# Cross attention with the queries on partitions: maxima from the scores themselves, weights transposed by DMA

## What is computed

```
xn = layernorm(ctx[b])                       # 1444 x 128
q  = (layernorm(x1[b]) @ Wq) * (1+scale) + shift
k, v = split(xn @ Wkv)
p  = softmax(q_h . k_h * 64**-0.5)            # for each head h: 100 x 1444
out = concat_h(p @ v_h) @ Wout;   x2[b] = layernorm(x1[b] + out)
```

## Time and profile before

| | us |
|---|---|
| median of 3 runs | 1530.29 (1527.89 to 1530.91) |
| profiled execution, its own time | 1527.42 |
| its span (first to last instruction) | 1525.6 |
| TensorE busy | 1356.7 (89%) |
| VectorE busy | 1162.8 (76%) |
| ScalarE busy | 857.3 (56%) |
| GpSimd busy | 625.4 (41%) |

### The profile page before, as it was taken

How to read it: one execution, slowest core, us unless ns; L and a number is a source line. 1 busy time by engine, 2 the same in 40 slices (tenths; PEclk the granted TensorE clock), 3 DMA queues, 4 the chain that set the end, 5 groups by cost and what they waited for, 6 DMA issues and landing times. The chain is left out here.

```text
span 1525.6 us, 28851 instructions
## 1 busy us (share of the span) xinstructions
PE 1356.7 (89%) x9254; PEld 835.3 (55%) x9254; DVE 1162.8 (76%) x3204; ACT 857.3 (56%) x1346; POOL 625.4 (41%) x419
## 2 busy tenths in 40 slices
PE   2769999999999999999999999999999753888888
PEld 2644555555555555555555555555555452777778
DVE  5967787777877787787777777777876328999994
ACT  0445676757667675767667575757665553222221
POOL 3243654636463554646364554636463300000010
PEclk9768999999999999999999999999999966666666
DMA  6020110101010110101010010101010110000000
GB/s 135 1 41 1 41 41 1 42 3 41 1 41 22 22 41 2 42 1 41 2 41 26 17 42 1 41 3 22 1 22 1 41 51 0 2 5 5 5 5 9
DMA packets 67469, 34.32 MB, mean 22 GB/s; under 512 B 53332, under 2 KB 64888, under 8 KB 67192
## 3 DMA queue, kind: packets, MB, share of 16 engines
q1 hardware_dynamic: 67320, 32.33, 9.2%
HBM read 18.92 MB, written 0.82 MB: 13 GB/s over the span
## 5 line engine op out<-in xcount | busy, mean ns | idle before, releaser
L800 POOL TENSOR_TENSOR p_lo<-e,p_hi 128x800 f16<-128x800 f32 x208 | 386.2, 1864 | 437.6 <-ACT p_hi L881 436.7
L928 DVE TENSOR_REDUCE mxp<-ps 128x1 f32<-128x481 f32 (+3 forms) x624 | 398.2, 654 | 153.1 <-PE ps L1040 141.4
L878 ACT ACTIVATE e<-ps 128x800 f32<-128x800 f32 (+1 forms) x384 | 324.7, 846 | 217.3 <-PE ps L1084 217.2
L881 ACT ACTIVATE p_hi<-ps 128x800 f16<-128x800 f32 (+1 forms) x384 | 325.2, 847 | 0.0
L1097 PE MATMUL ps<-p_hi,xa_hi 128*128 128x400 f16 (+1 forms) x768 | 256.3, 334 | 8.2 <-ACT p_hi L881 6.4
L1082 PE MATMUL ps<-q_hi,xT_hi 128*128 128x400 f16 (+1 forms) x768 | 257.6, 335 | 5.3 <-ACT p_hi L881 4.5
L1083 PE MATMUL ps<-q_lo,xT_hi 128*128 128x400 f16 (+1 forms) x768 | 256.0, 333 | 0.0
L1084 PE MATMUL ps<-q_hi,xT_lo 128*128 128x400 f16 (+1 forms) x768 | 256.0, 333 | 0.0
L1101 PE MATMUL ps<-p_lo,xa_hi 128*128 128x400 f16 (+1 forms) x768 | 255.1, 332 | 0.3
L1098 PE MATMUL ps<-p_hi,xa_lo 128*128 128x400 f16 (+1 forms) x768 | 255.1, 332 | 0.0
L1040 PE MATMUL ps<-xT_hi,q_hi 128*128 128x481 f16 (+3 forms) x624 | 236.4, 379 | 6.4 <-DMA xT_hi<-xa_hi 2.2
(11 more groups left out here) (223 smaller groups left out, 1948.0 us busy)
## 6 DMA issues: line engine op xcount, KB each, us to landing
raw<-in_ctx SPq DMA_DIRECT2D x16, 704.0 KB
f_wq<-in_L_ffn_w_q SPq DMA_DIRECT2D x1, 1024.0 KB, 6.3
f_wqt<-in_ffn_wq_t SPq DMA_DIRECT2D x2, 512.0 KB, 7.8
x_tok<-in_x SPq DMA_DIRECT2D x1, 800.0 KB
out_x<-ost SPq DMA_DIRECT2D x6, 128.0 KB, 1.9
wk_t<-in_wk_t SPq DMA_DIRECT2D x1, 512.0 KB, 5.9
wq_t<-in_wq_t SPq DMA_DIRECT2D x1, 512.0 KB, 8.2
wv_t<-in_wv_t SPq DMA_DIRECT2D x1, 512.0 KB, 10.5
```

The lines of the kernel that those rows point to most:

```text
L800: pool.tensor_tensor(out=p_lo[t % P_SLOTS][0:r, :, :], in0=e32[t % E_SLOTS][0:r, :, :], in1=p_hi[t % P_SLOTS][0:r, :, :], op=ALU.subtract) ...
L878: act.activation(e32[t % E_SLOTS][0:r, :, :], s_banks(t, r), ACT.Exp).then_inc(exp_done, 1)
L881: act.activation(p_hi[t % P_SLOTS][0:r, :, :], s_banks(t, r), ACT.Exp).then_inc(exp_done, 1)
L928: dve.tensor_reduce(mxp[0:r, mt, c:c + 1], src[0:r, 0:MCUT[c + 1] - MCUT[c]], AX_X, ALU.max).then_inc(work_dve, 1)
```

## The change

The queries go on partitions. A batch has 13 query tiles (NM), 12 of 128 queries and a last one of 64; the last computes the scores of 128 but uses only partitions 64 to 127. One tile's scores are 128 queries x 1444 keys in three PSUM banks (two sets of three), so VectorE reduces the maximum along the free direction from the scores themselves, adds 6.0 and ScalarE takes the exponent with this as its bias, once, as fp32. The high half is a copy of it, the low half the difference as before (GpSimd for tiles 1, 4, 7, 10, else VectorE). High and low half stand in one buffer `p` of 128 x 3072, which one transposing DMA turns into `pT`, 24 blocks with the keys on partitions. The values then take 36 matmuls of 128 columns a tile, five tiles behind the scores, in one bank; a copy to `uT` is made for every four tiles. The side work for the maxima is gone, queries and outputs use one bank. The loop is gone too: all 208 tiles are written out. Cut to its core:

```diff
-    body(Batch(None, 0), True, False)
-    with eng.Fori(0, (B - 2) // 2) as i:
-        body(Batch(i, 1), False, False)
-        body(Batch(i, 2), False, False)
-    body(Batch(None, B - 1), False, True)
...
+LAG = 5
+RING = 6
+E_BUF, P_BUF, N_BUF = 2, 3, 4
+GT = 4
+POOL_LO = (1, 4, 7, 10)
+Q_SLOTS = (2, 3, 7, 8)
+Y_SLOTS = (9, NM, NM + 1, NM + 4, NM + 5, NM + 6)
...
+            def turn_weights(t):
+                rows = tile_rows(t % NM)
+                sp.wait_ge(lo_pool if t % NM in POOL_LO else lo_dve, lo_of(t))
+                if t >= RING:
+                    sp.wait_ge(pv_done, t - RING + 1)
+                sp.dma_start_transpose(pT[:, t % RING, :, 0:rows.stop - rows.start],
+                                       p[t % P_BUF][rows, :, :].rearrange("q h k -> q (h k)")).then_inc(pT_ld[t % RING], 16)
...
+            for t in range(ALL_TILES):
+                b, i = divmod(t, NM)
+                turn_weights(t)
+                if i == 6 and b + 3 < B:
+                    sp.wait_ge(xh_done, b + 2)
+                    context_load(sp, cx, a, Batch(None, b + 3))
+                if i == 7 and b + 1 < B:
+                    turn_context(b + 1, 0, xa_hi_done)
+                if i == 8 and b + 1 < B:
+                    turn_context(b + 1, 1, xa_lo_done)
...
+            def low_half(t):
+                rows = tile_rows(t % NM)
+                pool.wait_ge(hi_done, t + 1)
+                pool.tensor_tensor(out=p[t % P_BUF][rows, 1, 0:T], in0=e32[t % E_BUF][rows, :], in1=p[t % P_BUF][rows, 0, 0:T],
...
+            def exponent(t):
+                rows = tile_rows(t % NM)
+                act.wait_ge(bias_done, t + 1)
+                if t >= E_BUF:
+                    act.wait_ge(lo_pool if (t - E_BUF) % NM in POOL_LO else lo_dve, lo_of(t - E_BUF))
+                act.activation(e32[t % E_BUF][rows, :], score_banks(t)[rows, 0:T], ACT.Exp,
+                               bias=bias[rows, t % N_BUF:t % N_BUF + 1]).then_inc(e_done, 1)
+
+            def high_half(t):
+                rows = tile_rows(t % NM)
+                if t >= P_BUF:
+                    act.wait_ge(pT_ld[(t - P_BUF) % RING], 16 * ((t - P_BUF) // RING + 1))
+                act.wait_ge(e_done, t + 1)
+                act.activation(p[t % P_BUF][rows, 0, 0:T], e32[t % E_BUF][rows, :], ACT.Copy).then_inc(hi_done, 1)
...
+            for t in range(ALL_TILES + DRAIN):
+                b, i = divmod(t, NM)
+                if t < ALL_TILES:
+                    exponent(t)
+                v = t - LAG
+                if 0 <= v < ALL_TILES and group_end(v):
+                    take_values(v)
+                asked = [j for j in jobs_of(t - 1) if j[0] == "q"] if t else []
+                for _, of, g in asked:
+                    take_queries(of, g)
+                if t < ALL_TILES:
+                    high_half(t)
+                for _, of, g in asked:
+                    queries_hi(of, g)
+                if i == 7 and b + 1 < B:
+                    context_hi(act, cx, Batch(None, b + 1))
...
+            def maximum(t):
+                rows, k = tile_rows(t % NM), t % N_BUF
+                dve.wait_ge(s_rdy, t + 1)
+                if t >= N_BUF:
+                    dve.wait_ge(e_done, t - N_BUF + 1)
+                dve.tensor_reduce(nmax[rows, k:k + 1], score_banks(t)[rows, 0:T], AX_X, ALU.max, negate=True).then_inc(max_done, 1)
+                dve.wait_ge(max_done, t + 1)
+                dve.tensor_scalar(bias[rows, k:k + 1], nmax[rows, k:k + 1], HEADROOM, None, ALU.add).then_inc(bias_done, 1)
...
+            for t in range(ALL_TILES + DRAIN):
+                b, i = divmod(t, NM)
+                if t < ALL_TILES:
+                    maximum(t)
+                if 0 < t <= ALL_TILES and (t - 1) % NM not in POOL_LO:
+                    low_half(t - 1)
+                for kind, of, g in jobs_of(t - 1) if t else []:
+                    if kind == "Y":
+                        take_heads(of, g)
+                if b + 1 < B:
+                    if i < 4:
+                        context_stats(dve, cx, Batch(None, b + 1), i)
+                    if i in (5, 6, 7):
+                        context_norm(dve, cx, Batch(None, b + 1), i - 5)
+                if i == 8 and b or t == ALL_TILES + DRAIN - 1:
+                    layer_norm(b - 1)
...
+            def scores(t):
+
+                b, i = divmod(t, NM)
+                if i == 0:
+                    pe.wait_ge(q_lo_done, 4 * (b + 1))
+                    pe.wait_ge(xT_ld, 32 * (b + 1))
+                if t >= 2:
+                    pe.wait_ge(e_done, t - 1)
...
+                for c in range(0, T, 512):
+                    keys = slice(c, min(c + 512, T))
+                    out = score_banks(t)[:, keys]
+                    pe.matmul(out, hi, xT_hi[b % 2][:, keys], start=True, stop=False)
+                    pe.matmul(out, lo, xT_hi[b % 2][:, keys], start=False, stop=False)
+                    last = pe.matmul(out, hi, xT_lo[b % 2][:, keys], start=False, stop=True)
+                last.then_inc(s_rdy, 1)
+
+            def values(t):
+
+                b, i = divmod(t, NM)
+                pe.wait_ge(pT_ld[t % RING], 16 * (t // RING + 1))
+                if i % GT == 0 and t:
+                    pe.wait_ge(u_done, group_number(t))
...
+                for n in range(NTILE):
+                    hi, lo = xa_hi[b % 2][:, n, :], xa_lo[b % 2][:, n, :]
+                    ph, pl = pT[:, t % RING, n, 0:w], pT[:, t % RING, NTILE + n, 0:w]
+                    pe.matmul(out, hi, ph, start=n == 0, stop=False)
+                    pe.matmul(out, lo, ph, start=False, stop=False)
+                    last = pe.matmul(out, hi, pl, start=False, stop=n == NTILE - 1)
+                last.then_inc(pv_done, 1)
...
+            for t in range(ALL_TILES + DRAIN):
+                if t < ALL_TILES:
+                    scores(t)
+                if 0 <= t - LAG < ALL_TILES:
+                    values(t - LAG)
+                for j in jobs_of(t):
+                    job(*j)
```

More of the change, by code:

```diff
@@ L24 @@
 HQ = H * S
-HALF = HQ // 2
-CH = HALF // 2
+PW = NTILE * P
 NM = (HQ + P - 1) // P
@@ L589, in context_lo @@
     if bt.off >= 2:
-        pool.wait_ge(c.pv_done, bt.val(2 * NTILE, -2 * NTILE))
+        pool.wait_ge(c.pv_done, NM * (bt.off - 1))
     pool.tensor_tensor(out=c.xa_lo[bt.par][:, :, :], in0=c.xh[:, :, :], in1=c.xa_hi[bt.par][:, :, :],
                        op=ALU.subtract).then_inc(c.xa_lo_done, 1)
[L595 to L624, removed]
@@ L627 @@
[L627 to L680, removed]
@@ L683 @@
[L683 to L700, removed]
@@ new lines, in tile_first_query, with lo_of, jobs_of @@
+def tile_first_query(i):
+    return min(i * P, HQ - P)
+def lo_of(t):
+    b, i = divmod(t, NM)
+    pool = b * len(POOL_LO) + sum(k <= i for k in POOL_LO)
+    return pool if i in POOL_LO else t + 1 - pool
+def jobs_of(t):
+    if t < 0:
+        return [("q", 0, g) for g in range(4)] if t == -1 else []
+    b, i = divmod(t, NM)
+    out = []
+    for g, s in enumerate(Y_SLOTS):
+        if i == s % NM and 0 <= b - s // NM < B:
+            out.append(("Y", b - s // NM, g))
+    for g, s in enumerate(Q_SLOTS):
+        if i == s and b + 1 < B:
+            out.append(("q", b + 1, g))
+    return out
@@ L707, in cross, with job_number, taken_of, group_end @@
+JOBS = [j for t in range(-1, ALL_TILES + DRAIN) for j in jobs_of(t)]
+def job_number(job):
+    return JOBS.index(job)
+def taken_of(k):
+    return sum(j[0] == JOBS[k][0] for j in JOBS[:k + 1])
+def group_end(t):
+    return t % NM % GT == GT - 1 or t % NM == NM - 1
+def group_number(t):
+    return t // NM * GROUPS + t % NM // GT
 def cross(nc, a, m, ps):
@@ L759, in _ @@
         @block.sync
         def _(sp):
[L761 to L776, removed]
+            def turn_context(b, half, made):
+                sp.wait_ge(made, b + 1)
+                if b >= 2:
+                    sp.wait_ge(s_rdy, NM * (b - 1))
+                dst, src = ((xT_hi, xa_hi), (xT_lo, xa_lo))[half]
+                sp.dma_start_transpose(dst[b % 2][:, :].rearrange("d (n q) -> d n q", q=P),
+                                       src[b % 2][:, :, :].rearrange("q n d -> q (n d)")).then_inc(xT_ld, 16)
@@ L1054, in work @@
+                else:
+                    need = NM * b + min(-(-(Y_HEADS[g][-1] + 1) * S // P), NM) - 1
+                    pe.wait_ge(u_done, group_number(need) + 1)
                     for j, h in enumerate(Y_HEADS[g]):
-                        last = pe.matmul(dst[0:S, j * (D + 1):(j + 1) * (D + 1)],
-                                         uT[half][:, :, :].rearrange("d c n -> d (c n)")[:, h * S:(h + 1) * S],
-                                         w2h[:, half * 8 + h, :], start=True, stop=True)
@@ L1105, in one_batch @@
-            def one_batch(bt, first, last):
-                w, nx = Works(bt, first, last), bt.next()
-                for u in range(2):
-                    for n in range(NTILE):
```

(30 more changed lines are left out.)

426 lines of the change are left out of this document (138 added, 288 removed).

## The result

The changed kernel takes 1827.43 us (median of 4, 1823.58 to 1829.08) against 1529.21 before: a ratio of 1.195, interval 1.192 to 1.197. I forecast 1461 us, faster; it is slower by a fifth, and beyond the 1711 of my slowest rival.

The account below looks back on a forecast made before the run. DMA was taken to bound at 59.9 us a batch, with 2 for clumps and 2 for GpSimd collisions about 64; 105 + 1019 + 21 + 311 gave a 1456 us span, 1461 us forecast, range 1385 to 1580.

Parts of the forecast that it names:

- slowest rival: Cross-stage transposes don't overlap: 5.6 us a weight tile, 79.7 a batch, 1711 us; chance 0.15, shared with DMA at 5.0 to 5.6.
- TensorE after: TensorE in the cross stage without maxima matmuls and turns: 55.2 us a batch, no longer bounding unless others are lower.
- How they meet: Engines' interplay in a cross-stage batch: 59.9 us of DMA, 2 for clumps, 2 for GpSimd collisions, about 64.
- my sum: Whole kernel: 105 + 1019 + 21 + 311 = 1456 us span, 1461 us as measured time.
- Prices: Cross-stage instruction times: reduction 1.66, difference 1.64, exponent 1.4 us to their ends, value matmuls 56 ns apart, landing alone 5.6 us.
- VectorE's sum: VectorE's work in the cross stage: 57.0 us a batch, with maximum and bias at 2.0 us a tile.
- That it would bound: DMA sets the cross stage's pace: 4.3 us a weight tile, 59.9 us a batch, bounds 56 and 65.
- my own sign: Cross-stage weight transposes: a landing time constant at 5.6 us with idle DMA between would refute the DMA bound.
- Start-up and tail: Around the cross stage: 19 us of start-up vanish, first scores at 105 us, last tile's tail 21 us.
- The lock rival: VectorE's one-element bias also waits for GpSimd: 68.4 us a batch, 1531 us, no change; chance 0.15.
- The lock itself: VectorE instructions with two SBUF inputs or two-port mode and GpSimd's exclude each other; 2 us a batch charged, at most 4.7.
- The clock: TensorE's cross-stage clock expected at 1.00; if it drops, the TensorE sum nearly doubles and the forecast is wrong.

Follow-up runs that it names:

- half of the transposes: Only the weights' high half transposed, read in place of the low half: changed kernel 1828.79 us, both takes first 1501.69, early-power kernel 1461.27.
- early-power kernel: Kernel with both takes first, plus GpSimd doing the context's power at tile 4 ahead of its difference: 1471.05 us, ratio to before 0.961.
- mended kernels: The kernel with both takes first (1505.36 us) and the early-power kernel (1471.05 us), each also run with half of the transposes.
- both takes first: Changed kernel, with VectorE taking heads before the maximum and ScalarE taking queries before the exponent: 1505.36 us, ratio to before 0.984.
- one slot moved: Last query job of a batch moved from tile 8 to 10: 1471.94 us on the kernel with both powers early, 1822.70 on the changed kernel.
- both powers early: Early-power kernel, plus the layer norm's power at tile 7 moved ahead of GpSimd's difference: 1469.70 us, ratio to before 0.960.

## Why the prediction was wrong

- **The step that failed** is "TensorE after" together with "How they meet": the queries and output products went into the sum with their matmuls, 2.1 and 4.2 us a batch, and of the ring between the engines I followed the score banks, the weight buffers and SyncE's queue, but not the bank of the side jobs. The two kernels have it in plain sight: `job` waits for the take of job k-1, where the kernel before, with two banks, waited for k-2; the takes stand behind the maximum or the exponent of a new tile; and in TensorE's queue the job stands ahead of the next scores. I never set the slots side by side. It measured 22.5 us a batch of waits. In TensorE's terms: the sum left it 8.8 us of a batch idle, and it was idle for 23.2; its matmuls were to take 55.2 at clock 1.00, and took 63.2 at 0.90. These 14.4 and 8.0 us are the 22.4 between my 64 and the measured 86.4; that the waits at jobs alone come to 22.5 as well is chance. Undoing it by order gave back 322 of the 366 us that the forecast was off.
- The rest of the error, 44 us: 34 were the context's power on GpSimd. I had counted its length, not its place behind a difference and a query half. The layer norm's, which looked the same, gave nothing back. With both kinds of order mended the change takes 1470 us, 0.6% above my sum, and that close fit is partly luck. The sum put 60 of its 64 us a batch down to DMA, and taking half of the transposes away from the early-power kernel changes it by 10 us in all.
- **Prices** held: reduction 1.661, difference 1.653, exponent 1.46, copy 1.41, GpSimd's difference 2.92 us, values 56 ns a matmul (the 36 of a tile start from 723.68 to 725.64, all with new weights), landing 5.6. VectorE's sum did not: I had 57.0 us a batch and it was busy for 52.3, above all since maximum and bias take 1.77 us start to start (723.88 to 725.65), not 2.0. ScalarE was busy for 46.0 (sum 43.4, with waits 46), GpSimd for 20.8 (I wrote 23, though my terms add up to 22.1). The groups of the page that answer to the earlier trace rows:

```profile
L874 DVE TENSOR_REDUCE nmax<-ps 128x1 f32<-128x1444 f32 (+1 forms) x208 | 345.1, 1659 | 523.6 <-PE ps L968 519.0
L809 ACT ACTIVATE e<-ps,bias 128x1444 f32<-128x1444 f32 (+1 forms) x208 | 304.3, 1463 | 582.6 <-DVE bias L876 582.3
...
L881 DVE TENSOR_TENSOR p<-e,p 128x1444 f16<-128x1444 f32 x144 | 238.3, 1655 | 3.8 <-ACT p L817 2.8
...
pT<-p SPq DMA_TRANSPOSE x208, 5.6
```

- **DMA**: 0.72 x 86.4 = 62 us a batch, where I had said 59.9. That it would bound was wrong in the changed kernel, by my own sign too: the landing is 5.6 us in the median, with the engines at 0.72. In the mended kernels half of the traffic was worth 4 and 10 us. The rival of transposes that don't overlap was wrong too, though its time lay nearest: the early-power kernel runs all of the transposes in batches of some 64 us. A number near the result is no proof of its mechanism.
- **Start-up and tail**: the 19 us of maxima went, as said, and the stretch 105 to 124 is part of the first tiles now. But the first scores start at 109.5 us, not at 105, having waited 3.15 us for GpSimd's low half of the queries; and from the last tile's scores (1488) to the feed-forward part (1516) it is 28 us, not 21.
- **The lock rival**: wrong in what it said of the bias, which took 150 to 155 ns in all 208 cases, also beside GpSimd, as in the first two lines, from the kernel with both takes first. The lock itself is there. In the changed kernel, in the last two lines, four pieces of the context norm beside GpSimd's difference of tile 7 take 3.71 us where they take 1.10 elsewhere:

```profile
622.62 2.92 POOL L773 TENSOR_TENSOR p<-e,p 128x1444 f16<-128x1444 f32 x1 [12.90 <-ACT p L817]
623.74 0.15 DVE L876 TENSOR_SCALAR bias<-nmax 128x1 f32<-128x1 f32 x1
...
774.48 3.71 DVE L564 TENSOR_SCALAR xh<-raw,cmv,crs 128x127 f32<-128x127 f32 x4
774.76 3.09 POOL L773 TENSOR_TENSOR p<-e,p 128x1444 f16<-128x1444 f32 x1 [16.35 <-ACT p L817]
```

In all the context norm takes 86.3 us there against 49.8 with both takes first: 2.3 us a batch. I had charged 2, but to the differences, of which none was held in the changed kernel (1.651 to 1.665 us). So the size came out near, in another place.

- **The clock**: I held that a fall would end the forecast, but looked for nothing that would bring it. It fell to 0.50 for stretches, as after the wait at 725.86 (mean 0.90), and came up to 0.96 when the waits were cut by order: 88 of the 320 us that this gave back, a second cost of the same step.

What stays open: the early-power kernel still has TensorE busy only 865 of 976 us with DMA at 0.98, VectorE at 0.84 and 81 us of query jobs waiting for ScalarE; half the transposes, one slot moved, or the second power changed it by 0.7% or less. Of VectorE's busy time with both powers early, some 78 us are longer rows beside GpSimd: 31.7 in the context norm, 23.1 in the layer norm, 23.5 in the 144 differences (261.8 us against 238.3 in the changed kernel). What they are worth was not tried. How much of TensorE's remaining waits a real second job bank would return was not tried, since all eight banks are in use.

The best version run, both takes first and both powers early, takes 1469.70 us, 4.0% less than the kernel before and 20% less than the change as made; with the context's power alone it is the same within the intervals.

## What to carry to other kernels

Before summing engines, list each shared bank or buffer with its depth before and after, and walk each ring through it in queue order: who must finish what before the next one may start. With a single bank, a side job in an in-order queue can wait for all that its taker does first; here letting the taker serve it first gave back 322 of 1827 us. When an edit takes a wait away and the time stays, look for the wait that grew, and for an instruction that now runs longer beside another engine's.

## Not expected of the hardware

- Issuing a full weight transpose held SyncE's queue 3.6 us (median of 208, up to 5.3), more than twice the 1.4 us of the half size (median of 208 with half of the transposes). The changed kernel takes the same time with either.
- The DMA engines at a share of 0.96 to 0.98 over a thousand microseconds did not set the time: halving the traffic was worth 4 us in one kernel and 10 us in the other.
- A one-element tensor_scalar on VectorE was not held by a GpSimd instruction (0.15 us inside one of 2.92), where the 100x128 one was the earlier trace rows, as were the 128x127 ones of the context norm (3.71 us for four instead of 1.10).
